# Two pre-norm transformer blocks in fp32: normalise steps, row shifts and division of attention outputs moved from VectorE to GpSimd, with a new written order for all engines

## The reference, cut to what matters

```python
x = x + attention(norm(x), W_qkv_a, b_qkv_a, W_out_a, b_out_a)
x = x + ffn(norm(x))
x = x + attention(norm(x), w_qkv_b, b_qkv_b, w_proj_b, b_proj_b)
x = x + ffn(norm(x))

def norm(x):      # eps = 1e-5
    return (x - mean(x)) / sqrt(var(x) + eps)
def attention(x, w_qkv, b_qkv, w_out, b_out):   # 16 heads of 32, causal
    q, k, v = split(x @ w_qkv + b_qkv)
    p = softmax(where(causal, q @ k.T * 32 ** -0.5, -inf))
    return (p @ v) @ w_out + b_out
def ffn(x):       # hidden size 2048
    return (silu(x @ w_gate.T) * (x @ w_up.T)) @ w_down.T
```

## Time and profile before

| what | value |
|---|---|
| median of 3 runs (lowest, highest) | 1995.39 us (1995.38, 1996.1) |
| the profiled execution: its own time, its span | 1995.06 us, 1993.3 us |
| busy: TensorE, VectorE, ScalarE, GpSimd | 98%, 60%, 40%, 49% |
| mean granted TensorE clock | 0.999 |
| attention stretch of the second iteration, 513.2 to 741.0 us | 227.8 us; TensorE 225.5 us busy, VectorE 156.6, ScalarE 130.2, GpSimd 73.2 |

### The profile page before, as it was taken

One profiled execution on the slowest core, in us unless ns is written; L12 is line 12 of the kernel. 1 busy time (PEld: TensorE's weight loads), 2 busy tenths in 40 slices (PEclk: granted clock), 3 DMA queues, 4 the chain that ended last, 5 costly groups with the idle time before them and its releaser, 6 DMA issues.

```text
span 1993.3 us, 27851 instructions
## 1 busy us (share of the span) xinstructions
PE 1957.7 (98%) x10288; PEld 1438.2 (72%) x10288; DVE 1188.4 (60%) x2387; ACT 803.7 (40%) x1478; POOL 983.5 (49%) x767
## 2 busy tenths in 40 slices
PE   6999999999999999999999999999999999999999
PEld 5655588888765558888875656888887565688887
DVE  4777465445578845544567884545456777554544
ACT  2388532221248752222115874222211687332221
POOL 4025369763212537975421252897532225289740
PEclk9999999999999999999999999999999999999999
DMA  5334011121333301311252340111113234012111
GB/s 139 90 86 111 3 55 62 54 64 32 72 82 93 97 21 44 106 45 62 74 138 65 86 97 23 42 64 54 53 32 96 65 86 97 12 53 64 53 43 42
DMA packets 58821, 132.37 MB, mean 66 GB/s; under 512 B 10560, under 2 KB 11584, under 8 KB 58688
## 3 DMA queue, kind: packets, MB, share of 16 engines
q1 hardware_dynamic: 58688, 130.60, 24.3%
HBM read 75.51 MB, written 4.19 MB: 40 GB/s over the span
## 4 chain that ended last, share of the span: by engine, by line
PE 87%; DVE 6%; issue 4%; ACT 2%; POOL 1%; DMA 1%; SPq 0%; DVEq 0%; POOLq 0%; ACTq 0%
PE bank L1488 11%; PE bank L1354 10%; PE bank L1356 10%; PE bank L1355 10%; PE ring L1354 9%; PE ring L1356 9%; PE ring L1355 9%; PE bank L1461 8%; PE ring L1430 8%; PE ring L1345 1%; DVE xn L1051 1%; ACT kq_parts L844 1%; DVE stats L1014 0%; POOL area L657 0%; DVE xt_lo L1060 0%
## 5 line engine op out<-in xcount | busy, mean ns | idle before, releaser
L732 POOL TENSOR_SCALAR_AFFINE_SELECT prob<-prob 128x512 f32<-128x512 f32 x128 | 83.7, 654 | 509.5 <-ACT prob L861 379.2
L861 ACT ACTIVATE prob<-bank 128x512 f32<-128x512 f32 (+1 forms) x512 | 271.8, 572 | 135.0 <-PE bank L1461 125.2
L1168 DVE TENSOR_TENSOR x<-x,bank 128x512 f32<-128x512 f32 x256 | 170.5, 685 | 232.3 <-PE bank L1356 231.7
L657 POOL TENSOR_TENSOR area<-w_stage,area 128x1024 fp32r<-128x1024 f32 x126 | 302.1, 2398 | 10.5
L655 POOL TENSOR_SCALAR area<-w_stage 128x1024 fp32r<-128x1024 f32 x126 | 144.3, 1145 | 301.1 <-PE bank L1356 189.7
L1098 DVE CUSTOM_DVE_ANT_0 xn<-ring,mask_row 128x384 bf16<-128x384 f32 (+7 forms) x384 | 244.9, 661 | 70.1 <-PE ring L1430 65.7
L1354 PE MATMUL ring<-xt_hi,area 128*128 128x512 f32 x672 | 263.9, 393 | 1.3 <-DVE area L1201 1.3
L1356 PE MATMUL ring<-xt_hi,area 128*128 128x512 f32 x672 | 262.1, 390 | 0.0
L1355 PE MATMUL ring<-xt_lo,area 128*128 128x512 f32 x672 | 262.1, 390 | 0.0
L1461 PE MATMUL bank<-area 98*128 98x512 f32 (+3 forms) x768 | 233.2, 372 | 2.3 <-DMA area<-nm_lo 1.4
L1430 PE MATMUL ring<-area 96*128 96x512 f32 (+3 forms) x768 | 221.7, 360 | 2.9 <-DVE row_max L1098 2.1
(11 more groups left out here) (171 smaller groups left out, 3643.9 us busy)
## 6 DMA issues: line engine op xcount, KB each, us to landing
w_stage<-ffn_w SPq DMA_DIRECT2D x96, 512.0 KB, 3.5
area<-kq_parts SPq DMA_DIRECT2D x336, 128.0 KB, 2.4
w_stage<-attn_w SPq DMA_DIRECT2D x32, 512.0 KB, 4.8
...
```

What stands on the lines that cost most here:

```text
L657: pool.tensor_tensor(lo, src, hi.bitcast(F32), ALU.subtract).then_inc(w_split, 1)
L861: act.activation(prob[:, step % PROB_BUFS, h, off:], scores_at(u, j, h), ACT.Exp, scale=SCALE).then_inc(prob_ready, 1)
L1168: dve.tensor_tensor(x[:, t, :], x[:, t, :], row_bank(s, n)[:, :], ALU.add).then_inc(rows_drained, 1)
```

## The change

The normalise step `(x - mean) * rstd` moves to GpSimd (`normalise_pair`), apart from the first four tiles of the kernel, which VectorE normalises pair by pair (`first_normalise`). The row shift of summed units moves to GpSimd and is now four steps instead of three. The product with the reciprocals moves to GpSimd for all divided units but the last. Each tile of x has its own semaphore, and at the start VectorE takes statistics tile by tile and passes on the variance after each pair; the low parts of the first two weight slots move from GpSimd to VectorE. There are three probability buffers instead of two and two masked buffers instead of three. The value tiles 0 and 1 lead the ring. All five strings are new. `WARM = 0` adds nothing. The diff, without most unchanged lines and without the parts that only adapt counts of semaphores:

```diff
...
-HEAD_OF_RING = (("q", 0), ("k", 0), ("v", 0), ("v", 1), ("ln1", 2), ("ln1", 3), ("q", 1), ("k", 1))
+HEAD_OF_RING = (("v", 0), ("v", 1), ("q", 0), ("k", 0), ("ln1", 2), ("ln1", 3), ("q", 1), ("k", 1))
...
-PROB_BUFS = 2
+PROB_BUFS = 3
...
+ATTN_ON_POOL = True
+SHIFT_ON_POOL = True
+WARM = 0
...
-    "pppppfffffffpfpppppfffffpppffpfpfpffpfpfpffpfpfpfpffpffpffpf",
-    "ssfpfssfssfsfsvsfsssfvffvvfsfvfsspffspffpff",
-    "ssvffsspfsfsvsfsfvffssvfssvfssvfssfvffssvfssfvssffvfssvssfssfvvsffsssv",
-    "ssfffsffssvffssfvfsspsssvvvfssfpffssvf",
-    "sspssffvfssfpfssfvffssvsfsffsfsfsfsvssffssvssffssvfssfssvssfssfv",
-    "ssffffsfsvsfsfsvfsfvsffvvsssppffpssssffvf",
-    "ssfvfsfsfsfpfssvsfsfsfvfsfsfsfsvfsfsfssfvsfsfsfssvsssffssssvfssf",
-    "svsfsfsvsfsfssfvvfssssvvssssv",
-    "ssfssvsfssvssvvssvssfsfssvvssvvssfssfssvvssssvvssssfvvf",
+    "fpfffffppffpppppffffppfpffpfppffpfpfpfpffppfppffpfpfpffpffpfpf",
+    "sffssfsfssfssfvssfsfvfsssfssfvvffvffpff",
+    "sspfssfpsfsfvsfsfpfsfsvfssvsfsfvssfvffssvsfsvsfsfsvvvsssffsvsfssfvvss",
+    "sffvvsffffssffssvfssfvfsppssspffpffssssfvvff",
+    "ssffvsffsfsfsvfsfsffsfsfsfsfvsfsfvssfvffssvsfsfsfsfssffssssvssfssfv",
+    "ssvvsfssffsvvsfppssspssffsspsfsfvv",
+    "sfsvsffsfsfsvffssffvsffsfsfsfsvfsfsfssfsfsvssffsvssffssssvvssssff",
+    "ssvsfsfsvsfssfssfssvvfssssvvvv",
+    "ssfssfssvssvssvssvssffssfssfssvvvvvssfssfssssvssssvvvv",
...
-    "xxxxxxx",
-    "eexeeeeeeeeexe",
-    "eeeeoeeexeeeeeeeeereereererereereerreer",
-    "eerrrxexeeoerererreeee",
-    "eeeexeeoxeeeeeeeeeereeeereereereereerrr",
-    "exerxeeoereererrrrreeexe",
-    "eeeoeexeeeeeeeeeeeeeeeeeeeeeee",
-    "eeeeeeoeeeeee",
-    "eeeeoeeeeeeeeeeeeeeeeeeeeeeeeoxx",
+    "xxxxxxxx",
+    "eeeeeeeeeeee",
+    "eeeeeexeeoxeeeeeeeereeeereeerrerererererr",
+    "ereroxeexeererrereexxee",
+    "eeeeeeeeoeereerererreereeerereexreexeeerer",
+    "eeoeerreerrereexeexe",
+    "eeeeeeoeeeeeeeeeeeeeeeeeeeeee",
+    "eeeeeeeeoeeeeo",
+    "eeeeeeeeeeeeeeeeeeeeeeeeeeeexox",
...
-    "mnnnnmnmnnmmmqmqmmqmmmmqmmmmmmmmqmqmmmmmmmqmmmqmmmmmmmmmmmmmmmmmmqmmrmqmmmmmmmmmmrmrmmrmmmmmrrrmrmmmmrmr"
-    "hmrmrrrmmrmrmmmmqmmqmrmmmmmrmrmmrrmmmrmmmrmrmmmmmmmmmhmmmmmmmmmqrmmrqrmrmmrmmrmmrmmmmmmmrmmmmmmmmmmrrrrr"
-    "rrrmmmmnnnrrrrrrrrlmm",
+    "nnmnnnmmmmmqmqmmmmmmmmqmmmqmmmmqmqmmmmqmmmmmmmqmmmmmmmmmmmmmmmmmqmmmqmrrrrmmrmmmmmrrmrmmmmmmmmrrmrrrmmmm"
+    "mmmrrmmrmqmmmmqmmmmmmmmmmmrmmmrmrmmmrrmrrrmmmmmmmmmqmmqmmmmmmmmmrmmmmrmmmmmmmrrmmrrmmrrmmmmmmmmrrrrrrrrm"
+    "mmmnrrrrrrrrlmm",
...
-    "dbbwmmmbmmwmmbmmmmmwmmmbwmmmmmwbaaawammmambmmmbamammdmmwdw",
+    "dbddwmmbmmbwmmmmtmbmhmwmtbwmtmmmbmbhmmaambawwammmmmtammmatamdddmmmwwd",
...
-    "klkkklkklkkmkkkkmkkmkkkklkmkkkklmkklkkkmkkklmlkml",
+    "kklkkkkkmkkkklmkkkklkmkkklkmklkkkmkkkklmkkmllkkml",
...
-MASKED_BUFS = 3
+MASKED_BUFS = 2
...
-        x_loaded = [sem(f"x_loaded{c}") for c in range(CHUNKS)]
+        x_loaded = [sem(f"x_loaded{t}") for t in range(TT)]
...
                 for t in range(c * CT, (c + 1) * CT):
-                    sp.dma_start(x[:, t, :], x_in[batch, t * P:(t + 1) * P, :]).then_inc(x_loaded[c], 16)
+                    sp.dma_start(x[:, t, :], x_in[batch, t * P:(t + 1) * P, :]).then_inc(x_loaded[t], 16)
...
             def inverse_deviation(it, ln, c):
-                n = it * 2 * CHUNKS + ln * CHUNKS + c + 1
-                pool.wait_ge(var_ready, n)
+                pool.wait_ge(var_ready, deviations(it, ln, c))
...
+            def normalise_attn(it, u):
+                g, c = unit(u)
+                cols = slice(c * CHUNK, (c + 1) * CHUNK)
+                pool.wait_ge(recip_done, evacuations(it, u) * RECIPS)
+                pool.tensor_tensor(attn[:, g, cols], attn[:, g, cols], recip[:, :], ALU.mult).then_inc(attn_ready, 1)
+            def normalise_pair(it, ln, r):
+                if r >= 2:
+                    pool.wait_ge(ring_full, full(it, (f"ln{ln + 1}", r - 2)))
+                pool.wait_ge(rstd_ready, deviations(it, ln, 2 * r // CT))
+                for t in (2 * r, 2 * r + 1):
+                    src = x[:, t, :] if ln else source_tile(it, t)
+                    pool.tensor_scalar(xn_tile(t), src, mean_var[:, t, 0:1], rstd[:, t:t + 1], ALU.subtract, ALU.mult
+                                       ).then_inc(xn_ready, 1)
+            def shift(it, u):
+                least = row_max[:, u % 2, :]
+                pool.wait_ge(inverse_done, shifts(it, u))
+                pool.tensor_tensor(row_inv[:, :], row_inv[:, :], row_sum[:, :], ALU.mult)
+                pool.tensor_tensor(row_log[:, :], least, row_log[:, :], ALU.subtract).then_inc(shift_step, 1)
+                pool.wait_ge(shift_step, 2 * shifts(it, u) - 1)
+                pool.tensor_tensor(row_log[:, :], row_log[:, :], row_inv[:, :], ALU.subtract).then_inc(shift_step, 1)
+                pool.wait_ge(shift_step, 2 * shifts(it, u))
+                pool.tensor_scalar(least, row_log[:, :], 1.0, None, ALU.add).then_inc(shift_ready, 1)
...
+            for r in range(2):
+                pool.wait_ge(var_ready, r + 1)
+                t = slice(2 * r, 2 * r + 2)
+                pool.tensor_tensor(rstd[:, t], var_eps[:, t], minus_half[:, 0:2], ALU.pow).then_inc(rstd_ready, 1)
+            pool.wait_ge(rstd_ready, 2)
...
-            inverse_deviation(0, 0, 0)
-            pool.wait_ge(xn_ready, CT)
-            for i in V_SLOTS:
-                hi, lo = w_part(i, slice(0, SLOT))
-                pool.wait_ge(w_hi_done, i + 1)
-                pool.tensor_tensor(lo, w_stage[:, i, :], hi.bitcast(F32), ALU.subtract).then_inc(w_split, 1)
+            pool.wait_ge(w_split, len(V_SLOTS))
...
-                deviations = iter(((0, 1), (1, 0), (1, 1)))
+                norms = iter((("deviation", 0, 1), ("pair", 0, 2), ("pair", 0, 3), ("deviation", 1, 0),
+                              ("pair", 1, 0), ("pair", 1, 1), ("deviation", 1, 1)))
+                shifted = iter(SUMMED)
+                divided = iter([u for u in PLAIN if ATTN_ON_POOL and u != UNITS - 1])
...
+                    elif what == "h":
+                        shift(it, next(shifted))
+                    elif what == "t":
+                        normalise_attn(it, next(divided))
                     else:
-                        inverse_deviation(it, *next(deviations))
+                        name, *which = next(norms)
+                        if name == "pair":
+                            normalise_pair(it, *which)
+                        else:
+                            inverse_deviation(it, *which)
+                normalise_pair(it, 1, 2)
+                normalise_pair(it, 1, 3)
...
+                normalise_pair(it + 1, 0, 0)
+                normalise_pair(it + 1, 0, 1)
...
-                dve.wait_ge(stats_done, 2 * n - CT)
-                for t in range(c * CT, (c + 1) * CT):
+                variances(n, range(c * CT, (c + 1) * CT))
+            def variances(n, tiles):
+                dve.wait_ge(stats_done, 2 * n - len(tiles))
+                for t in tiles:
...
-                t = slice(c * CT, (c + 1) * CT)
+                t = slice(tiles[0], tiles[-1] + 1)
...
+            def first_normalise(r):
+                dve.wait_ge(rstd_ready, r + 1)
+                for t in (2 * r, 2 * r + 1):
+                    dve.tensor_scalar(xn_tile(t), x[:, t, :], mean_var[:, t, 0:1], rstd[:, t:t + 1],
+                                      ALU.subtract, ALU.mult).then_inc(xn_ready, 1)
+            def first_weights_lo(i):
+                hi, lo = w_part(i, slice(0, SLOT))
+                dve.wait_ge(w_hi_done, i + 1)
+                dve.tensor_tensor(lo, w_stage[:, i, :], hi.bitcast(F32), ALU.subtract).then_inc(w_split, 1)
...
-                if t == CT and it == 0:
-                    dve.wait_ge(x_loaded[1], 16 * CT)
+                if it == 0:
+                    dve.wait_ge(x_loaded[t], 16)
...
-                if it == 0:
-                    dve.wait_ge(x_loaded[c], 16 * CT)
-                elif first_layer(it):
+                if first_layer(it):
...
-            def normalise_pair(it, ln, r):
-                if r >= 2:
-                    dve.wait_ge(ring_full, full(it, (f"ln{ln + 1}", r - 2)))
-                dve.wait_ge(rstd_ready, it * 2 * CHUNKS + ln * CHUNKS + 2 * r // CT + 1)
-                for t in (2 * r, 2 * r + 1):
-                    src = x[:, t, :] if ln else source_tile(it, t)
-                    dve.tensor_scalar(xn_tile(t), src, mean_var[:, t, 0:1], rstd[:, t:t + 1],
-                                      ALU.subtract, ALU.mult).then_inc(xn_ready, 1)
...
-                def shift(u):
-                    least = row_max[:, u % 2, :]
-                    dve.wait_ge(inverse_done, shifts(it, u))
-                    dve.tensor_tensor(row_inv[:, :], row_inv[:, :], row_sum[:, :], ALU.mult)
-                    dve.tensor_tensor(row_log[:, :], least, row_log[:, :], ALU.subtract).then_inc(shift_step, 1)
-                    dve.wait_ge(shift_step, shifts(it, u))
```

(29 more changed lines are left out.)

11 lines of the change are left out of this document (6 added, 5 removed).

## The result

The changed kernel takes 2051.53 us (median of four runs, 2049.44 to 2054.5) against 1995.39 (1994.24 to 1996.1): a ratio of 1.0283, 95% interval 1.0267 to 1.0299. It is slower by 56 us; the forecast was 35 us faster. The profiled execution has a span of 2047.7 us, before 1993.3.

A forecast was written before the change was run, and what follows sets the result against it. TensorE, busy 98% of the span, was taken as the bound, with only order, waits and matmul spacing movable. Terms 4.7 + 5.4 + 2.3 + 4.4 + 9.6 + 9 = 35.4 us off 1995.06 gave 1960 us, range 1943 to 1986.

The forecast's parts named there:

- two tiles at 0.62 each: Second half of each iteration's first normalise: GpSimd makes a normalised tile in 0.62 us, so the chain ends at 522.4.
- safety bound: First normalise: even at 1.3 us per GpSimd tile the chain ends at 523.8, before TensorE's need at 525.3.
- Start: Kernel start: first real matmul at 13.3 instead of 17.98, gaining 4.7 us, bounds 2.5 and 5.5.
- rival B: Added GpSimd work slows VectorE's remaining steps, leaving 1 to 4 of 9 us in the attention stretch: 1965 to 1968, chance 0.13.
- first matmul of an iteration: Iteration boundaries: the ring's value tile goes first and avoids the wait for a bank, gaining 3 × 0.78 = 2.3 us.
- late pairs: Second normalise: moving its late pairs to GpSimd brings hidden products sooner and ends TensorE's ring-buffer wait, gaining 4.4 us.
- first-normalise stops: Second half of each iteration's first normalise: TensorE's four stops of 1.36 us disappear, gaining 5.4 us.
- written order: TensorE's order strings: 47 instead of 55 runs of weigh steps per iteration, 0.3 us each, gaining 9.6 us, bounds 5 and 12.
- attention waits: Attention stretch: VectorE's relief and a third probability buffer save 2.25 us per iteration, 9 us in all.
- C, the late row shift: Summed units: the row shift stands late in GpSimd's queue, eight stops of 6 us, giving 2008; chance 0.10 with all else slower.
- waits for GpSimd's products, masks or shifts appear among TensorE's: Failure sign: TensorE's list of waits would show it waiting for these GpSimd steps.
- an attention stretch not at least 3 us shorter: Failure sign for the attention stretch, 513.2 to 741.0 before, which was forecast to shorten by about 6 us.

The follow-up runs named there:

- after_multadd: The changed kernel with GpSimd's normalise step written as multiply then add, at the same place of its queue: 2000.84 us.
- new_norm_dve: The changed kernel with its normalise steps back on VectorE, where the kernel before had them in VectorE's order: 1999.42 us.
- new_norm_dve_sp: The changed kernel with normalise steps on VectorE and weight loads in SyncE's string moved behind the stacking transfers of units 4, 5 and 7: 1976.96 us.
- repaired kernels: Versions of the changed kernel with SyncE's weight loads behind stacking transfers and GpSimd's fill after the first four normalised tiles; with normalise on VectorE 1973.22 us.
- best_stop: The repaired kernel with normalise on VectorE, plus added TensorE waits before score tiles of unit 3 in iterations 1 to 3: 1976.33 us.
- The best kernel: The changed kernel with normalise steps on VectorE, weight loads behind stacking transfers in SyncE's string, and GpSimd's fill after the first four normalised tiles: 1973.22 us.
- new_all_dve_sp_fill: The repaired kernel with normalise steps, products with the reciprocals and row shifts all on VectorE: 1979.78 us.

## Why the prediction was wrong, by its own steps

**The step that failed** is the price in "two tiles at 0.62 each (a GpSimd tensor_scalar of this size)". The row it came from, L751, is a step with two constants, multiply then add; the normalise step subtracts first and takes both scalars from memory. Its price is 2.08. With that price the prediction's own chain for the first normalise turns: its safety bound, "if a tile cost 1.3, 523.8 is still early", was against a need of 525.3, and two tiles at 2.08 end at 522.4 + 2.9 = 525.3, with no slack, and the second pair of the chunk 4.2 us after that. That second pair is the one for which TensorE then stopped, 11.4 us in four iterations. The larger part, 16.8 us, are stops for the first two pairs of the second normalise, and for them the sum had no term: before, TensorE did not wait there (243.31 to 247.26), and the prediction moved these steps without working out their time. I also tested the unknown step only up to the price of its dearest neighbour in sight, a two-input step at 1.3. The row gave an operation's name and shape and hid the two operations inside it; nothing in the trace of before bounded this one from above. after_multadd shows that this price, and not the place in the queue, was nearly all of it: with the same steps at the same places, 50.7 of the 56 us come back.

The Trainium skill (GPSIMD Engine Reference, Engine selection) calls two-input steps some two times slower on GpSimd and one-input steps roughly line-rate. By that the normalise step would have been harmless; measured, one-input steps of 128x512 lie between 0.62 and 2.08 us there, against 0.50 on VectorE. Its advice to keep elementwise work on VectorE held for this step as it was written; in its cheap form the step cost next to nothing on GpSimd (1975.35 against 1973.22), and the products and shifts gained 6.6 us there.

**What no term had: the clock.** I priced a stop of TensorE at its length. Here a stop of one to three microseconds was often followed by 3.4 to 13.7 us at the lower clock level. new_norm_dve still has three half-clock stretches of 3.4 us: two behind stops for L898 (1.9 and 2.3 us), one behind a stop of 1.4 us for a stacking transfer. With those stops gone (new_norm_dve_sp) these three are gone, though one of 6.8 us behind a 1.0 us stop is new. Of the repaired kernels with normalise steps in time three have none, and best_stop has one of 3.4 us. The length of a stop alone does not decide it: the longest stop of new_norm_dve, 2.8 us at 1614.3, and one of 2.7 us at 1148.9 in the changed kernel have no slow stretch behind them, and the ten stops of 0.8 to 1.2 us after the start of the kernel before have none. That a stop costs more than itself rests on these pairs of kernels and on the window rows; best_stop, meant to test it alone, made no stop long enough, and what decides whether the clock falls stays open.

*Start*, 4.7 us: the chain was right up to the first pair, and the first real matmul is at 13.51 (forecast 13.3) once the fill is moved. What I missed is in my own sentence, that the power is "now ahead of GpSimd's long fill": then the fill lies beside VectorE's second pair, 4.72 us in place of 1.00. I had the mechanism as rival B and counted it only in the attention stretch. The Trainium skill (GPSIMD Engine Reference, Key points) says that GpSimd shares its SBUF interfaces with VectorE and contends with its instructions that are in a two-port mode or have two inputs; the trace agrees that the two engines contend, 4.72 us beside the fill against 1.00 away from it, but does not show in which mode the step ran.

*Outside the attention stretches*, the first matmul of an iteration and the late pairs, 2.3 + 4.4 = 6.7 us: right. The best kernel gains 21.6 us of span, of which 4.5 are the start (first real matmul 17.98 to 13.51) and 9.9 the attention stretches (913.6 to 903.7 us in sum); the other 7.2 lie here. The changed kernel itself gained 8.1 here, 2.0 an iteration, as "the rest of an iteration by 2" said. (The 913.6 counts the old kernel's stretches to the end of its string, a transpose that follows the last weigh step; to the last weigh step they are 910.5.)

*Inside them*, the first-normalise stops, the written order and the attention waits, 5.4 + 9.6 + 9 = 24.0 us: too high by far. The stops are gone in the best kernel, so of its 9.9 us they are 5.4 by the prediction's own count, and some 4.5 are left for order and waits together, a quarter of 18.6. Without GpSimd's help the stretches lose only 5.8 (new_all_dve_sp_fill, 907.8). What the fewer runs, the buffers and the relief give one by one, no run separates. And the order had a cost that I didn't look for: I counted runs in TensorE's string, and did not look at which of ScalarE's steps now come right behind the DMAs that they wait for. That cost 22.5 us, more than the order gained. It would have been found by listing, for each DMA, what is issued just ahead of it on its queue and which step of which engine needs it next, in both strings.

*Rivals.* C, the late row shift, was the one on the slower side, at 0.10; the result lies on that side by another mechanism. The signs named for a failure, "waits for GpSimd's products, masks or shifts appear among TensorE's", left out the one GpSimd step that turned up there. The other sign, an attention stretch not at least 3 us shorter, did show: the second was 15 us longer.

*Sum for the changed kernel*, from the runs: the order, the buffers, the relief and the new start would give −22 (1973.22 against 1995); the fill at the start +3.7, the string +22.5, the normalise step on GpSimd +52. That makes 2051.4, measured 2051.53. That it closes is no proof, since the three prices are the differences between kernels on the way from one to the other, and so must close; what it shows is their sizes. Taken off in another order, with string and fill mended first, the form costs 54.6.
